# Attention copies of q and k in two halves by heads: where ScalarE issues the first half

## The reference, cut to what matters

```
x = x + cross_attention(layernorm(x), ctx)        # 16 heads of 64, 64 context tokens
n = layernorm(x)
q, k, v = n @ wq, n @ wk, n @ wv                  # 16 heads of 16
scores = (q . k) / sqrt(16), causal; attn = softmax(scores) @ v
h = n + rmsnorm(attn @ wo);  ffn = silu(h @ w1) * (h @ w3) @ w2
dense = h + rmsnorm(ffn)
sparse = rmsnorm(top-2 of 8 experts on n)
x = x + dense + sparse
```

## Time and profile before

| | |
|---|---|
| median of 3 runs | 1483.63 us |
| span of the profiled execution | 1484.5 us |
| TensorE matmul, busy | 1362.4 us, 92% |
| VectorE | 810.0 us, 55% |
| ScalarE | 575.1 us, 39% |
| GpSimd | 600.2 us, 40% |
| mean granted clock of TensorE | 0.976 |
| TensorE waiting for the copies | 17.8 us, 7 times |

### The profile page before, as it was taken

The page is one execution under the profiler, slowest core; times in us unless marked ns, Lnnn a source line. Parts: engine busy times, 40 slices in busy tenths (PEclk is TensorE's granted clock), DMA queues, the critical chain, the costliest instruction groups (busy, mean ns, idle before and its releaser), DMA issues. The chain is left out here.

```text
span 1484.5 us, 22385 instructions
## 1 busy us (share of the span) xinstructions
PE 1362.4 (92%) x7229; PEld 882.2 (59%) x7230; DVE 810.0 (55%) x1654; ACT 575.1 (39%) x1214; POOL 600.2 (40%) x1051
## 2 busy tenths in 40 slices
PE   6887899899999989998999899999999889999995
PEld 5543556666665666566656665666566346666674
DVE  2625554764585368536753675467537623333348
ACT  2231553055306521642265126503640443344446
POOL 4312353254325342634254225423542445555544
PEclk9998899999999999999999999999999899999997
DMA  6053204110501050106000500140022533322245
GB/s 213 1 153 132 86 1 121 52 30 1 142 30 30 1 156 16 30 8 160 20 15 30 141 17 15 51 121 17 1 83 74 162 107 128 129 87 85 85 186 193
DMA packets 78297, 115.39 MB, mean 78 GB/s; under 512 B 24840, under 2 KB 66208, under 8 KB 75648
## 3 DMA queue, kind: packets, MB, share of 16 engines
q1 hardware_dynamic: 67888, 79.69, 17.9%
q10 hardware_dynamic: 3840, 16.78, 4.2%
q0 software_dynamic: 6480, 17.77, 3.3%
HBM read 70.22 MB, written 43.59 MB: 77 GB/s over the span
## 5 line engine op out<-in xcount | busy, mean ns | idle before, releaser
L1540 DVE TENSOR_REDUCE nm<-ps 128x2 f32<-128x256 f32 (+3 forms) x256 | 202.5, 819 | 85.6 <-PE ps L970 79.5
L1229 ACT ACTIVATE room<-ps 128x512 f32<-128x512 f32 x320 | 179.8, 599 | 151.3 <-PE ps L996 151.1
L1051 PE MATMUL ps<-hT,w 128*128 128x512 f32 x768 | 206.5, 412 | 0.0
L703 POOL TENSOR_SCALAR_AFFINE_SELECT room<-room 128x256 f32<-128x256 f32 (+1 forms) x320 | 121.0, 390 | 136.4 <-ACT room L1229 131.7
L969 PE MATMUL ps<-room 96*128 96x128 bf16 (+3 forms) x512 | 127.9, 312 | 35.7 <-DMA room<-parts_d 17.8
L1051 PEld LDWEIGHTS ps<-hT,w 128*128 128x128 f32 x768 | 140.4, 190 | 32.1 <-DVE hT L1570 2.0
L1061 PE MATMUL ps<-w,room 128*128 128x256 f32 x512 | 137.8, 400 | 7.8 <-DVE room L1591 7.8
L1253 ACT ACTIVATE room<-ps 128x512 f32<-128x512 f32 x64 | 37.2, 593 | 277.2 <-PE ps L1051 277.2
L1087 PE MATMUL ps<-room 128*128 x284 | 135.4, 599 | 1.8 <-ACT room L1281 1.8
L920 PE MATMUL ps<-room 128*128 128x256 f32 x512 | 123.1, 384 | 2.8 <-ACT room L1190 1.8
L901 PE MATMUL ps<-room,xnT 128*128 128x512 f32 x256 | 122.0, 601 | 0.0
(11 more groups left out here) (236 smaller groups left out, 2360.1 us busy)
## 6 DMA issues: line engine op xcount, KB each, us to landing
room<-parts_d SPq DMA_DIRECT2D x48, 256.0 KB, 8.7
room<-parts_d ACTq DMA_DIRECT2D x48, 256.0 KB, 6.2
room<-xs_d SPq DMA_DIRECT2D x71, 129.0 KB
parts_d<-room SPq DMA_DIRECT2D x64, 128.0 KB, 1.8
room<-pair_d SPq DMA_DIRECT2D x8, 1024.0 KB, 7.8
room<-in_L_ffn_ew SPq DMA_DIRECT2D x24, 256.0 KB, 5.5
xin<-in_x SPq DMA_DIRECT2D x8, 512.0 KB, 11.3
parts_d<-xnT SPq DMA_DIRECT2D x32, 128.0 KB, 1.8
```

Source lines behind the costliest of these rows:

```text
L703: done(g.affine_select(out=w, in_=w, compare_op=ALU.is_ge, fill=0.0, base=0, pattern=[[0, 2]] * (blocks - 1) + [[1, P]], channel_multiplie ...
L1051: last = mm(bank(up_banks(b, m)[i]), w[:, x, k, m * P:(m + 1) * P], hT[:, y, k, :], start=((x, y, k) == terms[0]), stop=((x, y, k) == term ...
L1229: done(fn(prob[:, u * 512:(u + 1) * 512], bank(score_bank(b) + n % 2), ACT.Exp), "b_exp")
L1540: done(v.tensor_reduce(nm[:, t, 2 * hp:2 * hp + 2], pair_ps, AX.X, ALU.max, negate=True), "a_max")
```

## The change: the copies in two halves

The heads are taken in two halves of eight. The four projections now run in the order q half 0, k half 0, q half 1, k half 1 (QK). parts_d is laid out half by half, so that head h stands at place h of the copies and rep_at is gone. The semaphores q_out, k_out, rep_q, rep_k (six stores or six loads each) become out_0, out_1 (six stores each) and rep_0, rep_1 (twelve loads each), by half. The storing queue stores the first half's six parts, waits for them, issues k's first half, stores the second half's six parts, waits, and issues both second halves, q's and then k's, and only then loads x. ScalarE issues q's first half at "v" 0, before xk, and no copies at "route" 0. Max 0 waits for rep_0, max 16 for rep_1. Instead of 12 loads of 256 KB there are 24 of 128 KB.

```diff
+QK = ((0, 0), (1, 0), (0, 1), (1, 1))
...
-        parts_d = internal("parts_d", (3, 2, HD, H // KD, KD, S), BF16)
+        parts_d = internal("parts_d", (3, 2, KD, HD, H // KD, S), BF16)
...
+        def copy_part(eng, which, a):
+
+            rows = slice(a * (H // KD), (a + 1) * (H // KD))
+            for j in range(NREP):
+                src = parts_d[(Q_PART, K_PART)[which][j], which, a, :, :, :].rearrange("d h n -> d (h n)")
+                done(eng.dma_start((q_rep, k_rep)[which][j:KREP:NREP, rows, :].rearrange("d h n -> d (h n)"), src), ("rep_0", "rep_1")[a], 16)
...
+            def send_parts(b, half):
+                for n in (2 * half, 2 * half + 1):
+                    which, a = QK[n]
+                    for i, name in enumerate(("part1", "part2", "part3")):
+                        need(sp, b, name, n + 1)
+                        done(sp.dma_start(parts_d[i, which, a, :, :, :].rearrange("d h n -> (d h) n"), parts[i][:, n, :]), ("out_0", "out_1")[half], 16)
...
-                    for a in range(4):
-                        for i, name in enumerate(("part1", "part2", "part3")):
-                            need(sp, b, name, a + 1)
-                            done(sp.dma_start(parts_d[i, a // 2, :, :, a % 2, :].rearrange("d h n -> (d h) n"), parts[i][:, a, :]), ("q_out", "k_out")[a // 2], 16)
+                    send_parts(b, 0)
...
-                    need(sp, b, "k_out", per["k_out"])
-                    for j in range(NREP):
-                        src = parts_d[K_PART[j], 1, :, :, :, :].rearrange("d h a n -> d (h a n)")
-                        done(sp.dma_start(k_rep[j:KREP:NREP, :, :].rearrange("d h n -> d (h n)"), src), "rep_k", 16)
+                    need(sp, b, "out_0", per["out_0"])
+                    copy_part(sp, 1, 0)
+                    send_parts(b, 1)
+                    need(sp, b, "out_1", per["out_1"])
+                    copy_part(sp, 0, 1)
+                    copy_part(sp, 1, 1)
...
-                            need(pe, b, "rep_q", per["rep_q"])
-                            need(pe, b, "rep_k", per["rep_k"])
+                            need(pe, b, "rep_0", per["rep_0"])
...
+                        if nmax == H // 4 * T:
+                            need(pe, b, "rep_1", per["rep_1"])
...
                         if t == 0:
+                            if c is not None:
+                                need(act, c, "b_ps", per["b_ps"])
+                            need(act, b, "out_0", per["out_0"])
+                            copy_part(act, 0, 0)
                             need(act, b, "xn2", T)
...
                     elif kind == "route" and step[1] == 0:
-                        if c is not None:
-                            need(act, c, "b_ps", per["b_ps"])
-                        need(act, b, "q_out", per["q_out"])
-                        for j in range(NREP):
-                            src = parts_d[Q_PART[j], 0, :, :, :, :].rearrange("d h a n -> d (h a n)")
-                            done(act.dma_start(q_rep[j:KREP:NREP, :, :].rearrange("d h n -> d (h n)"), src), "rep_q", 16)
                         need(act, b, "gmax", 1)
```

More of the change, by code:

```diff
@@ L56 @@
     qk_ps=4, part1=4, rest1=4, part2=4, part3=4, v_ps=4, v_sb=4, lg=4,
-    q_out=96, k_out=96, rep_q=96, rep_k=96, z=1,
+    out_0=96, out_1=96, rep_0=192, rep_1=192, z=1,
     gmax=1, gexp=1, mask=1, rank_ps=1, slot=1, xk=1, scat=128, dve_step=42, pool_a=4, pool_n=1,
@@ L185, in score_bank @@
     return 2 if b is None else 6
-def rep_at(h):
-    return h % (H // KD) * KD + h // (H // KD)
 def score_rows(u):
@@ L465, in send_shifts @@
                 for r in range(MROWS):
-                    done(sp.dma_start(q_rep[KREP + r:KREP + r + 1, rep_at(first_head):rep_at(end_head - 1) + 1:KD, :],
+                    done(sp.dma_start(q_rep[KREP + r:KREP + r + 1, first_head:end_head, :],
                                       mT[r * H + first_head:r * H + end_head, i, :]), f"m_row{i}", 16)
@@ L553, in batch @@
                     if c is None:
-                        need(sp, b, "q_out", per["q_out"])
                         need(sp, b, "pv_ps", per["pv_ps"])
@@ L932, in batch @@
                             need(pe, b, "xn2T", 2)
-                        w = (wq, wk)[a // 2]
+                        which, half = QK[a]
+                        w = (wq, wk)[which]
                         for k in range(KD):
-                            last = mm(bank(a), w[:, k, a % 2 * P:(a % 2 + 1) * P], xn2T[:, k, :], start=(k == 0), stop=(k == KD - 1))
+                            last = mm(bank(a), w[:, k, half * P:(half + 1) * P], xn2T[:, k, :], start=(k == 0), stop=(k == KD - 1))
                         done(last, "qk_ps")
@@ L968, in batch @@
                             o = nmax % 2 * 2 + i
-                            mm(bank(o, n), q_rep[0:KREP, rep_at(h), t * P:n], k_rep[0:KREP, rep_at(h), 0:n], start=True, stop=False)
+                            mm(bank(o, n), q_rep[0:KREP, h, t * P:n], k_rep[0:KREP, h, 0:n], start=True, stop=False)
                             last = mm(bank(o, P, t * P), ident_b[:, :], mask_qk[:, :], start=False, stop=True)
@@ L994, in batch @@
                             o = (score_bank(b) + n % 2) * 512 + at
-                            h = rep_at(4 * grp + j)
+                            h = 4 * grp + j
                             last = mm(ps[:, o:o + S - kb * P], k_rep[0:KREP + MROWS, h, kb * P:(kb + 1) * P], q_rep[0:KREP + MROWS, h, kb * P:S],
@@ L1195, in batch @@
                         need(act, b, "qk_ps", a + 1)
-                        done(fn(parts[0][:, a, :], bank(a), ACT.Copy, scale=(HD ** -0.5 if a < 2 else 1.0)), "part1")
+                        done(fn(parts[0][:, a, :], bank(a), ACT.Copy, scale=(1.0 if QK[a][0] else HD ** -0.5)), "part1")
                         if a >= 1:
@@ L1480, in batch @@
                             need(dve, b, "part3", a - 1)
-                        done(v.scalar_tensor_tensor(rest[:, a % 2, :], bank(a), (HD ** -0.5 if a < 2 else 1.0), parts[0][:, a, :], ALU.mult, ALU.subtract), "rest1")
+                        done(v.scalar_tensor_tensor(rest[:, a % 2, :], bank(a), (1.0 if QK[a][0] else HD ** -0.5), parts[0][:, a, :], ALU.mult, ALU.subtract), "rest1")
                     elif kind == "v":
```

## The result

The changed kernel takes 1503.22 us (median of 4 runs, 1500.19 to 1507.33) against 1483.93 before (1481.46 to 1485.07): ratio 1.013, 95% interval 1.0109 to 1.015. It is slower by 19.3 us, where 8.0 were forecast (1491.6, range to 1500.0). The profiled execution is the slowest of the four: 1507.33 us, its span 1505.6, so 21.1 above the span before.

A forecast was written before the change was run, and what follows sets the result against it. TensorE, busy 92% of the span, was taken as the bound. Batches +8.6, first walk −5.2 and clock +4.6 summed to +8.0 on the median of 1483.63, giving 1491.6 us, range 1479 to 1500.

The forecast's parts named there:

- hold ahead of fu, 7 batches: Before fu in each batch: ScalarE's six issues ahead of xk make fu start 4.1 us later; +28.7 over seven.
- fu to max at full clock: From first fu matmul to first max step: 14.3 us instead of 17.18 in each batch, −20.2 over seven.
- clock behind the idle: After the new idle before fu: clock falls in 3 of 4 batches at 2.0 us, +10.5 in all.
- clock given back: First max step to next xk copy: clock falls put down to the copy waits disappear with them, −5.9.
- first walk, first v matmul to first max step: In the first walk: the max step follows the slots at about 115.3 instead of 120.55, −5.2.
- The wait for the copies goes: At the first max step of batches 1 to 7: TensorE's wait for the copies, 17.8 us in all, disappears.
- fu starts 4.1 later: In each batch: 0.34 us wait for the store's landing, 3.71 for six issues and 0.05 delay fu.
- cheap issues: Rival at ScalarE's issues: each half costs 0.33 us, fu starts 2.6 late, 1476.0 us; chance 0.11.
- A fall in 3 of 4 batches at 2.0 us: After the idle of about 4 us before fu: TensorE's clock falls that often, +10.5 over seven batches.
- The rival of long falls: Rival behind the idle before fu: every clock fall is a long one, 2.7 us each, 1500.0 us; chance 0.13.
- The first walk's −5.2: In the first walk: k and v stores pass the later loads, so the first max step comes 5.2 us earlier.
- the first walk keeps its 120.5: Sign of a wrong forecast: the first walk's first max step stays at 120.5 instead of 115 to 116.

The follow-up runs named there:

- e5_fill: The changed kernel with four extra float32 matmuls on TensorE ahead of fu's wait for hT, results overwritten; 1489.88 us.
- e7_hold_first_walk: The changed kernel with ScalarE issuing q's first half ahead of xk in the first walk only, the storing queue issuing it in later batches; 1456.18 us.
- e6_three_issues: The changed kernel with ScalarE issuing three of q's six first-half copies ahead of xk and the storing queue the other three; 1479.72 us.
- e3_before_early_q: The kernel before, whole 256 KB copies, with only ScalarE's six issues of q moved from the route step to ahead of xk; 1498.40 us.
- e9_fill_two: The changed kernel with two extra float32 matmuls on TensorE ahead of fu's wait for hT; 1491.43 us.

## Why the prediction was wrong

The direction and the mechanism were right (the hold, which is the time that the six issues keep ScalarE, delays fu, and the clock falls behind the idle); the size was less than half. The step that failed most is the clock's: falls in 3 of 4 batches at 2.0 us, +10.5. All seven fell, for +15.1. By the prediction's own steps, in the profiled executions:

| term | forecast | measured | from |
|---|---|---|---|
| hold ahead of fu, 7 batches | +28.7 | +32.4 | six stretches 757.73 − 735.82 + 5.9 of clock; first max step to batch 1's fu, 129.72 − 125.15 = +4.6 |
| fu to max at full clock | −20.2 | −21.9 | 98.37 (e5_fill) − 120.25 |
| clock behind the idle | +10.5 | +15.1 | 113.43 − 98.37 |
| clock given back | −5.9 | −5.9 | all six stretches at 1.00 |
| first walk, first v matmul to first max step | −5.2 | −4.1 | 28.04 (120.93 − 92.89) − 32.14 (120.55 − 88.41) |
| ahead of that v matmul | 0 | +4.5 | 92.89 − 88.41 |
| behind the last max step | 0 | +1.0 | 363.0 − 362.0 |
| sum | +8.0 | +21.1 | |

The first two forecasts add up to 8.5; the recorded sum has 8.6 for them.

- **The wait for the copies goes: right.** The slots release every first max step now. The second halves and x cost nothing either: no wait for them among TensorE's.
- **"fu starts 4.1 later": right in kind, 0.5 short in each batch, 3.7 in all.** In batch 2 six issues took 3.97, one of them 0.86 while both engines issued. Issue cost independent of bytes was right; cheap issues were not.
- **"A fall in 3 of 4 batches at 2.0 us": the step that failed most, by 4.6.** All seven fell, at 15.1 / 7 = 2.2 each. The rival of long falls, at 1500.0, came nearest in the number, but with 2.7 for each fall it had the size wrong. Why before three waits of six were followed by a fall and here all seven were stays open.
- **The first walk's −5.2: right in mechanism, 1.1 short.** The 6.75 us wait for a store is gone and the max step follows the slots. But the slots come 1.15 us later than before, counted from the first v matmul (88.41 in the kernel before): the hold, put at "about as much as the old one", costs 1.2 more (e7_hold_first_walk). The changed kernel:

```profile
92.89 1.05 PE L951 MATMUL ps<-wv,xn2T 128*128 128x264 f32 x4
...
120.70 0.17 DVE L1541 COPY room<-ids_all 128x4 uint32<-128x4 uint32 x1
...
120.93 0.23 PE L979 MATMUL ps<-room 96*128 96x128 bf16 x1 [1.20 <-DVE room L1541]
```

```profile
88.41 1.05 PE L942 MATMUL ps<-wv,xn2T 128*128 128x264 f32 x4
```

- **The first max step at 120.93 doesn't speak against that.** The prediction named "the first walk keeps its 120.5" as a sign of being wrong, and it came, but from 4.5 us ahead of the first v matmul, before any copy is issued (95.46). 2.9 of them lie ahead of the q and k projections: the first of these (L944) starts at 82.89 against 80.03 before. The other 1.6 lie in the projections, at a low clock (0.53 from 82 to 86 us). The clock from 20 to 40 us is lower too than the 0.91 of before:

```profile
20.00:40.00 20.00, 17.05 (x93) 15.38 (x93) 7.63 (x21) 3.58 (x6) 2.39 (x4) 0.72 0.31 96
```

This belongs to the one profiled execution: in the ten profiled ones the first projection starts between 78.41 and 82.89, and e7_hold_first_walk, with the same instructions up to there, has its first max step at 116.48. What lowers the clock there was not followed up.

Without these 4.5 us the terms add up to 16.6; the medians differ by 19.3. The 2.7 between stay open, within the spread of the runs (7.1 us in the four of the changed kernel). A run's time has some 1.8 us that its span leaves out (1507.33 against 1505.6), so the profiled execution of the kernel before, with its span of 1484.5, was by this estimate slower than the four runs given above, and not 0.9 above their median as the prediction has it. Its sum doesn't rest on that.

The fall in all seven batches is what the Trainium skill's rule on idle ("TensorE: Matmul & The Clock Gate", Why this matters for your kernels) would have given, at 14.0 instead of my 10.5; the measured 15.1 agrees. That issuing is usually small beside the transfer, as the Trainium skill has it ("DMA: Bandwidth & Descriptors", Issuing engines are not separate DMA queues), fits only part of the trace: an issue on ScalarE took 0.61 us (median), against 0.53 for moving 128 KB at the rate of the earlier trace rows, though 4.5 (median) from issue to landing in the changed kernel. What it costs lies elsewhere, in the work behind it on ScalarE: three issues fewer take 14.1 us of TensorE's idle away (31.4 to 17.3, e6_three_issues).

## What to carry to other kernels

Before a transfer's issue is moved ahead on a compute engine, follow what stands behind it on that engine: here six issues of 0.6 us, whose bytes did not matter, stood in front of hT, and 39 us hung on their place. A gap on the engine that sets the time can cost more than its length: here 31.4 us of idle brought another 15.1 through the clock behind it, while 7.6 us in shorter gaps (e5_fill) brought none. Give the issues to an engine that computes nothing: so placed, the same change is 2% faster than the kernel before.

## What the runs showed of the hardware

- An issue into every sixth of 96 partitions took 0.59 us from SyncE and 0.61 from ScalarE (medians), with 8 KB or 16 KB per row. In the changed kernel single ones took up to 1.0 on ScalarE and 1.4 on SyncE.
- Falls of the clock by idle ahead of full work: 4.2 to 5.1 us, 14 of 14 (changed kernel, e3_before_early_q); 2.5 us, 6 of 7 (e6_three_issues); 2.7 to 3.6 with filled work ahead, 3 of 7 (e9_fill_two); 0.9 to 1.9, 0 of 7 (e5_fill). Useless matmuls held it up and saved 13 us.
- Between 1.6 and 3.8 us length alone does not decide. In the kernel before, the stretch behind a wait of 3.23 us kept its clock and the one behind 2.34 us did not:

```profile
548.74 0.22 PE L969 MATMUL ps<-room 96*128 96x128 bf16 x1 [3.23 <-DMA room<-parts_d]
979.55 0.22 PE L969 MATMUL ps<-room 96*128 96x128 bf16 x1 [2.34 <-DMA room<-parts_d]
```

```profile
548.74:670.40 121.66, 117.88 (x703) 76.31 (x704) 71.84 (x129) 49.49 (x99) 50.21 (x77) 1.00 0.08 25
979.55:1102.82 123.27, 119.49 (x703) 77.23 (x704) 71.83 (x129) 49.48 (x98) 50.18 (x77) 0.99 0.06 21
```
